# Two layers of feed-forward on one Trainium2 core: one TensorE product group started earlier, and a new order at the end

## The reference, cut to what matters

```python
# _L1_cond_ref: 1376 hidden values, LoRA of rank 16 chosen per batch row
gate = lora_add(einsum('bnh,fh->bnf', x, W_gate), x, A_gate, B_gate)
up   = lora_add(einsum('bnh,fh->bnf', x, W_up),   x, A_up,   B_up)
act  = silu(gate) * up
down = lora_add(einsum('bnf,hf->bnh', act, W_down), act, A_down, B_down)
# _L1_ffn_ref
xn = down * rsqrt(mean(down*down) + EPS)
xq = round(xn * 127 / max|xn|), clipped, / scale      # per token
wq = ternary weights
y  = xq @ wq.T + b
return x + (down + gelu(y))                           # the outer sum adds x
```

## Time and profile before

| | |
|---|---|
| median of 3 runs | 1114.65 us |
| lowest, highest | 1109.14, 1114.69 us |
| the profiled execution, its own time | 1114.94 us |
| its span, first to last instruction | 1113.1 us |
| TensorE busy | 1048.8 us (94%) |
| VectorE, ScalarE, GpSimd busy | 621.8, 336.2, 106.6 us |
| mean granted TensorE clock | 0.985 |
| share of TensorE in the chain that ended last | 86% |

### The profile page before, as it was taken

The page is one execution under the profiler, slowest core; times in us unless marked ns, Lnnn a source line. Parts: engine busy times, 40 slices in busy tenths (PEclk is TensorE's granted clock), DMA queues, the critical chain, the costliest instruction groups (busy, mean ns, idle before and its releaser), DMA issues.

```text
span 1113.1 us, 13813 instructions
## 1 busy us (share of the span) xinstructions
PE 1048.8 (94%) x5412; PEld 881.7 (79%) x5416; DVE 621.8 (56%) x797; ACT 336.2 (30%) x539; POOL 106.6 (10%) x161
## 2 busy tenths in 40 slices
PE   0899999999999999999889999999999999999976
PEld 0788888778888888888778888888888888788753
DVE  8864477876656574544764523533433433555686
ACT  1432132334333332312441212212212212224544
POOL 4500000000000000000120101001001001111122
PEclk9899999999999999999999999999999999999996
DMA  3676130010101011200410211201201201221012
GB/s 104 224 247 233 51 121 1 1 57 1 57 0 57 0 57 38 97 36 13 142 59 15 85 29 57 85 28 57 85 28 56 85 28 51 91 58 44 33 57 85
DMA packets 27338, 73.78 MB, mean 66 GB/s; under 512 B 5346, under 2 KB 5538, under 8 KB 27170
## 3 DMA queue, kind: packets, MB, share of 16 engines
q1 hardware_dynamic: 21794, 49.65, 12.6%
q0 software_dynamic: 5504, 23.60, 7.0%
HBM read 66.79 MB, written 6.44 MB: 66 GB/s over the span
## 4 chain that ended last, share of the span: by engine, by line
PE 86%; DVE 8%; issue 2%; DMA 2%; ACT 2%; POOL 0%; DVEq 0%; ACTq 0%; POOLq 0%
PE ps_g L184 18%; PE ps_g L185 18%; PE ps_g L186 18%; PE ps_d L184 9%; PE ps_d L185 9%; PE ps_d L186 9%; DMA lr_raw<-in_tab_l,rows 2%; PE ps_d L992 1%; PE ps_g L1024 1%; DVE acc L2127 1%; PE ps_g L888 1%; DVE tmp L1530 1%; DVE ar_lo L1988 0%; DVE b_lo L2045 0%; ACT a_hi L1335 0%
## 5 line engine op out<-in xcount | busy, mean ns | idle before, releaser
L184 PE MATMUL ps_g<-a_hi,gu_hi 128*128 128x512 f32 x544 | 216.9, 399 | 3.0 <-DVE a_lo L1663 2.2
L185 PE MATMUL ps_g<-a_lo,gu_hi 128*128 128x512 f32 x544 | 213.8, 393 | 0.0
L186 PE MATMUL ps_g<-a_hi,gu_lo 128*128 128x512 f32 x544 | 213.4, 392 | 0.0
L184 PEld LDWEIGHTS ps_g<-a_hi,gu_hi 128*128 128x128 f32 x544 | 103.3, 190 | 22.3 <-DVE a_lo L1663 2.3
L186 PEld LDWEIGHTS ps_g<-a_hi,gu_lo 128*128 128x128 f32 x544 | 103.1, 190 | 22.4
L2025 DVE TENSOR_TENSOR s_act<-s_act,ps_g 128x512 f32<-128x512 f32 x44 | 30.3, 688 | 160.6 <-PE ps_g L186 159.9
L185 PEld LDWEIGHTS ps_g<-a_lo,gu_hi 128*128 128x128 f32 x544 | 103.4, 190 | 18.5
L1352 ACT ACTIVATE h_hi<-s_act 128x512 fp32r<-128x512 f32 x44 | 27.8, 631 | 152.0 <-DVE s_act L2025 152.0
L371 POOL DMA_INDIRECT lr_raw<-in_tab_l,rows x40 | 38.3, 957 | 351.7 <-PE ps_g L888 327.0
L184 PE MATMUL ps_d<-dn_hi,h_hi 128*128 128x512 f32 x176 | 69.5, 395 | 2.0 <-DVE h_lo L2029 2.0
L1346 ACT ACTIVATE s_act<-ps_g 128x512 f32<-128x512 f32 x43 | 25.7, 598 | 144.4 <-PE ps_g L186 144.4
(11 more groups left out here) (314 smaller groups left out, 2256.9 us busy)
## 6 DMA issues: line engine op xcount, KB each, us to landing
raw<-in_w SPq DMA_DIRECT2D x25, 768.0 KB, 5.7
toep_hi<-krev_hi SPq DMA_DIRECT2D x12, 512.0 KB, 5.6
toep_lo<-krev_lo SPq DMA_DIRECT2D x12, 512.0 KB, 6.7
acc<-in_x_t SPq DMA_DIRECT2D x4, 1024.0 KB, 11.1
out<-x1b SPq DMA_DIRECT2D x16, 256.0 KB, 2.0
toep_lo<-krev_hi SPq DMA_DIRECT2D x4, 512.0 KB, 6.2
w_all<-in_wq SPq DMA_DIRECT2D x1, 1024.0 KB, 6.4
kept_hi<-a_hi SPq DMA_DIRECT2D x2, 512.0 KB, 8.1
```

The lines of the kernel that those rows point to most:

```text
L184: pe.matmul(out_ap, st_hi, mv_hi, start=start, stop=False, skip_group_check=skip)
L185: pe.matmul(out_ap, st_hi, mv_lo, start=False, stop=False, skip_group_check=skip)
L186: return pe.matmul(out_ap, st_lo, mv_hi, start=False, stop=stop, skip_group_check=skip)
```

## The change

In the half chunk, for the last tile, TensorE issues the 12 main matmuls of the first full chunk's up products (slot 0, tile 0, into `ps_gu[1]`) ahead of `down_part`. The loop body becomes a function `full_chunk(c, up_begun)`; the first full chunk is written out with `up_begun = True`, where the up group of tile 0, slot 0 is only its 6 LoRA matmuls, and the hardware loop runs over the other three.

At the end, TensorE's list after the last `lora_hidden` was: `lora_rows(3)`, `quantised(2)`, `x_rows(3, 0)`, `x_rows(3, 1)`, products 8 and 9, `quantised(3)`, products 10 to 15. It becomes: `quantised(2)`, `lora_rows(3)`, products 8 to 11, `x_rows(3, 0)`, `quantised(3)`, `x_rows(3, 1)`, products 12 to 15. VectorE's list is reordered as the diff shows. ScalarE, GpSimd and SyncE have the same lists as before.

```diff
--- before.py
+++ after.py
@@ -953,12 +953,15 @@
                 for t in range(NT):
                     if t + 1 < NT:
                         half_gate(t + 1)
+                    else:
+                        pe.wait_ge(s_wlg[0], NC0 + 1)
+                        gate_up_main(ps_gu[U_BANK[0]], 1, 0, 0)
                     down_part(1, NC0, t, M1 + t, True).then_inc(s_d[1], 1)
                     pe.wait_ge(r_adl, t + 1)
                     lora_hidden(((1, t % 2),), M1 + t)
                     if t + 1 < NT:
                         half_up(t + 1)
-                with pe.Fori(NC0 + 1, CL) as c:
+                def full_chunk(c, up_begun):
                     for t in range(NT):
                         m = c * NT + t
                         r = c * NT + (t - M1)
@@ -971,7 +974,10 @@
                                 pe.wait_ge(s_silu[0], tiles(0, m) + 1)
                             else:
                                 pe.wait_ge(s_mul[0], tiles(0, m))
-                            gate_up(ps_gu[U_BANK[f]], 1, f, f, t, r + 1).then_inc(s_u[f], 1)
+                            if up_begun and t == 0 and f == 0:
+                                gate_up_rows(ps_gu[U_BANK[f]], 1, f, t, r + 1).then_inc(s_u[f], 1)
+                            else:
+                                gate_up(ps_gu[U_BANK[f]], 1, f, f, t, r + 1).then_inc(s_u[f], 1)
                             if f == 0:
                                 pe.wait_ge(q_tev, r + 1)
                                 transposes(ps_t, 2, r)
@@ -980,6 +986,10 @@
                         pe.wait_ge(r_adl, r + 1)
                         lora_hidden(((0, 0), (1, 1)), m)
 
+
+                full_chunk(NC0 + 1, True)
+                with pe.Fori(NC0 + 2, CL) as c:
+                    full_chunk(c, False)
 
                 def x_rows(t, half):
 
@@ -1092,14 +1102,14 @@
                     down_part(1, CL, t, m, False).then_inc(s_d[1], 1)
                     pe.wait_ge(r_adl, RL + t + 1)
                     lora_hidden(((0, 0), (1, 1)), m)
+                quantised(2)
                 lora_rows(3)
-                quantised(2)
+                for s in range(8, 12):
+                    product(s)
                 x_rows(3, 0)
+                quantised(3)
                 x_rows(3, 1)
-                product(8)
-                product(9)
-                quantised(3)
-                for s in range(10, NSUB):
+                for s in range(12, NSUB):
                     product(s)
 
             @block.scalar
@@ -2250,25 +2260,26 @@
                     if t == 2:
                         logits(3)
                 logits(7)
-                td_masked(3)
-                td_low(3)
                 for i in range(4):
                     quantise(2, i)
+                td_masked(3)
+                keep_quantised(2, 0)
+                td_low(3)
+                keep_quantised(2, 1)
+                whole(7)
                 fresh(3)
                 largest(3)
-                for j in range(2):
-                    keep_quantised(2, j)
+                logits(8)
+                logits(9)
                 factors(3)
-                whole(7)
-                logits(8)
                 for i in range(4):
                     quantise(3, i)
-                logits(9)
+                logits(10)
+                with_x(3, 0)
                 for j in range(2):
                     keep_quantised(3, j)
-                    logits(10 + j)
-                for half in range(2):
-                    with_x(3, half)
+                logits(11)
+                with_x(3, 1)
                 whole(11)
                 for s in range(12, NSUB):
                     logits(s)
```

## The result

| | before | after |
|---|---|---|
| median, 12 runs each | 1113.47 us | 1106.85 us |
| lowest, highest | 1107.80, 1115.70 us | 1104.91, 1117.48 us |
| profiled execution, span | 1113.1 us | 1105.6 us |
| mean granted clock in it | 0.985 | 0.990 |

A forecast was written before the change was run, and what follows sets the result against it. The prediction took TensorE as the bound, busy for 94% of the span and 86% of the chain. From the profiled 1114.94 us it took 1.45 and 5.2 us, giving 1108.3 us, range 1105.8 to 1113.2.

The forecast's parts named there:

- The time, the range, the sign: Whole kernel: 1108.3 us, range 1105.8 to 1113.2; faster by over 0.5% at chance 0.57, within 0.40, slower 0.03.
- The first edit, 1.45 us: Half chunk to first full chunk: early up products win 2.65 us on TensorE, of which 1.45 us stay.
- the new wait: Before the first full chunk's transposes: TensorE waits 1.2 us for VectorE's `ps_t` copy.
- The second edit, 5.2 us: Last part, reordered on TensorE and VectorE: last instruction ends at 1104.2 instead of 1109.40, saving 5.2 us.
- the stand before product 10: Last part: TensorE idle 3 us or more before product 10, released by `logits(8)`.
- Rival C: Last part only trades places, its gain being a clock gain; only the early up products count: 1113.5 us, chance 0.11.
- `x_rows` out of the chain: Last part: tile 3's `x_rows` half 1 leaves the chain altogether; one source of the 5.2 us.
- products 8 and 9 under `fresh`: Last part: products 8 and 9 run while VectorE does `fresh`; one source of the 5.2 us.
- no meeting with GpSimd: Last part: `quantise(3)` no longer runs beside GpSimd's sum, so 1 us comes back; one source of the 5.2 us.
- The written-out chunk: First full chunk written out ahead of the loop: costs nothing at run time, 0.5 us as upper end.
- Rival A: Last part: clock stays at 0.50 after TensorE's stand before product 10; 1114.1 us, chance 0.22 with its mixes.
- Rival B: Last part: half clock already from `quantised(2)` and `lora_rows(3)`, slower than before; 1115.3 us, chance 0.05.

The follow-up runs named there:

- Copy_first: Changed kernel with VectorE's copy of `ps_t` for the half chunk's last tile moved ahead of its LoRA row split; ratio to before 0.9916, median 1105.24 us.
- last_only: Kernel before with only the new order of TensorE and VectorE in the last part; ratio to before 0.9998, median 1115.26 us.
- peel_only: Kernel before with the first full chunk written out and the loop over three chunks, without early up products; ratio to before 0.9965, median 1108.21 us.
- shift_before: Kernel before with 11 useless matmuls on TensorE between the half chunk and the first full chunk; ratio to before 0.9996, median 1111.04 us.
- first_only: Kernel before with only the early up products and the written-out first full chunk, last part as before; ratio to before 0.9935, median 1108.12 us.
- after_filler: Changed kernel with useless matmuls: 5 ahead of `quantised(2)`, 4 ahead of `lora_rows(3)`, 15 ahead of product 10; ratio to before 0.9937, median 1106.33 us.
- after_again: The changed kernel, unaltered, measured a second time on another chip; ratio to before 0.9950, median 1107.20 us.
- fill_idle: Kernel before with 8 useless matmuls in TensorE's 1.95 us stand ahead of the half chunk's last down products; ratio to before 0.9978, median 1108.49 us.
- before_filler: Kernel before with useless matmuls in the last part, 11 ahead of `lora_rows(3)` and 6 ahead of `x_rows(3, 0)`; ratio to before 0.9971, median 1109.37 us.

## Why the prediction was right, and where it wasn't

*The time, the range, the sign*: right. 1108.3 for 1106.85, and "faster by over 0.5%" at a ratio of 0.9947; the interval, 0.9929 to 0.9965, has that border inside it. That the sum came so close is in good part luck. It was 1.45 us for the first edit and 5.2 for the second; measured by themselves, the first gave 6 to 7 us and the second none.

*The first edit, 1.45 us*: right in the trace as to its steps: both stands gone, the new wait of 1.05 us (forecast 1.2) by VectorE's `ps_t` copy; 11.87 to 10.16 us is 1.7, of which 0.24 came from an earlier split of the LoRA rows (616.18 is 6.02 us after the low part, 618.49 was 6.26). Copy_first shows the wait for what it is. What was missing is that the stand of 1.95 us brings a fall of the clock in some executions, another 0.9 us. The forecast named stands only as idle time there, though it had read the price of a fall at the other place.

*The second edit, 5.2 us*: this is the step that failed, by its size. Its mechanics came as written (start of `lora_rows(3)`, 4.4 us for it, the stand before product 10, the pieces of `quantise`, about 29 us, which came as 29.7 from the end of that `lora_hidden`). But the 34.5 us on the other side were one execution's. With the old order III was 34.5, 33.4, 34.1, 30.6 and 28.2 us in five traces without filling there, 32.2 in the mean; with the new order 29.9, 32.3, 28.4 and 28.4, in the mean 29.8. So it is worth about 2.4 us in the mean by these few traces (with a standard error of 1.5), nothing at full clock, and nothing in last_only's timing. The old order's III goes with its falls: 28.2 us with none, 30.6 in peel_only, with 3.4 us at half clock in `lora_rows(3)`, and 33.4 to 34.5 in the three traces with another 6.8 to 10.2 us from `x_rows(3)` on. Rival C had this in half a sentence ("the last part's gain is a clock gain") and got 0.11.

*Where the gain came from*: I named three causes, `x_rows` out of the chain, products 8 and 9 under `fresh`, and no meeting with GpSimd. At full clock the old order does without all three (28.2 us). They are costs of the executions in which the clock has fallen. The meeting of VectorE and GpSimd was real, 1.49 us for one piece and not 0.43, but three of the six traces with the old order, shift_before among them, don't have it. The Trainium skill, SBUF — State Buffer, section "SBUF: two separate sides", says that such a pair blocks, and the rows agree; they add that whether the two meet is a matter of where each stands.

*The written-out chunk*, a term that I put at nothing with 0.5 us as its upper end: no run bears the nothing out. peel_only, which has it alone, was 4.0 us faster than before in the mean (2 to 6 by its interval), so a part of what the first edit's timing shows may come with it.

*Rival A* is a fair description of last_only's trace, and in the changed kernel it came in part: the clock was back at 1.00 at 1089.9. The forecast read the price of a stand from the two that had a fall behind them; before's own trace also has stands of 1.95 us (ahead of 612.98) and 1.61 us (ahead of 1031.42) with none, and it didn't weigh those. *Rival B* had no case among the twelve runs of the change except perhaps one of 1117.48 us, at a mean clock of 0.979.

*What stays open.* The timing gives 6 to 7 us to the first edit alone and none to the second alone, the traces 1.4 to 2.6 and 0 to 2.4. More than half of the first may belong to the written-out chunk, whose matmuls are those of before, in their order; whether through the longer program or through where the falls come, no run separates. By the slope of 0.84 us, 2.4 of first_only's 6.4 us (its mean of 1108.25 against 1114.63) go with its higher clock (0.9897 against 0.9869), 4.0 don't, of which the trace shows 1.4. That a move of the work by 1 or 2 us changes where it is met by a fall is consistent with all of it, and shift_before (mean 0.5 us under before, instead of 2.0 over) leans that way, but its interval holds the opposite too. No run here settles it.

## What to carry to other kernels

When an engine with a clock that is granted stands, cost the stand twice: its length, and half speed for what follows, in the executions where its clock falls. Don't take the one profiled execution of before for the typical one in a stretch where the clock moved: look at that stretch in a few executions first, and ask what it takes at full clock, since that is what a new order must beat. And when an early start is bought with a new wait, look at once whether the releaser can be moved too: moving VectorE's copy cost two lines and gave back 1.0 to 1.1 us in stretch I.

## What the runs showed of the hardware

Kernels whose instructions up to 600 us are the same differ there. In twelve of the fourteen traces the clock first fell at 47.9 to 50.4 us and was back at 51.8 to 55.1; last_only and after_filler had no fall there but one that began at 228 to 229 us, and first_only and after_again had both. The half chunk's last low part came between 610.1 and 613.0 us. So 3 us of a difference between two profiled spans can be had with no change at all. The clock was at 0.50 or 1.00 of full speed (1.2 or 2.4 GHz). The Trainium skill, TensorE: Matmul & The Clock Gate, section "The HAM clock gate (the "warmup" mystery)", says that the array's rate is one of two and that the moment of a change varies from run to run; the fourteen traces agree, with no third value and with the starts above.

A fall began within 1.5 us of the end of the 1.95 us stand in three traces and not in two others; after the stand of 2.89 us it did so in before, first_only, fill_idle and peel_only, and not in shift_before. The new order's stand of 3.71 us had a fall that began in it or within 0.8 us behind it in all four traces that have it (after, last_only, copy_first, after_again). The stands of 0.7 and 1.0 us that end between 1055 and 1068 us had one behind them in last_only and before_filler and in none of the other twelve. The instructions just ahead of each of these stands were the same each time, so the length of a stand alone doesn't say whether the clock falls.

A VectorE `quantise` piece of 128 x 512 took 0.41 to 0.43 us in 221 of 224 cases, and 1.49 us in the three in which GpSimd's sum had begun up to 0.2 us before it.
